# A token-routed layer in tiles: six sets of tile buffers and a first group of one chunk

## The reference

```python
x = x + attn_a(layernorm(x))        # delta rule, a scan over the tokens
x = x + ffn(layernorm(x))
x = x + attn_b(layernorm(x))        # linear attention, in chunks, with a running state
x = x + ffn(layernorm(x))

def ffn(x):                         # 8 experts, 128 -> 256 -> 128, the best two of each token
    probs = softmax(x @ Wg); topw, topi = top_k(probs, 2); topw = topw / sum(topw)
    combine = sum(one_hot(topi, 8) * topw[..., None])
    y = relu(x @ W1[e]) @ W2[e]     # for every expert e
    return sum_e(combine[:, e] * y[e])
```

## Time and profile before

| | us |
|---|---|
| median of 3 runs (828.03 to 835.17) | 830.47 |
| the profiled execution, device time | 829.9 |
| its span, first to last instruction | 828.2 |
| PE busy of the span | 650.5 |
| DVE busy | 623.2 |
| POOL busy | 487.7 |
| ACT busy | 483.2 |

### The profile page before, as it was taken

One profiled execution on the slowest core, in us unless ns is written; L12 is line 12 of the kernel. 1 busy time (PEld: TensorE's weight loads), 2 busy tenths in 40 slices (PEclk: granted clock), 3 DMA queues, 4 the chain that ended last, 5 costly groups with the idle time before them and its releaser, 6 DMA issues.

```text
span 828.2 us, 16746 instructions
## 1 busy us (share of the span) xinstructions
PE 650.5 (79%) x5108; PEld 534.2 (64%) x5108; DVE 623.2 (75%) x1648; ACT 483.2 (58%) x1266; POOL 487.7 (59%) x552
## 2 busy tenths in 40 slices
PE   4744265998989899686755979998999999787694
PEld 3423143877767778475652757886888778677594
DVE  4598989999999999999995685776678766352314
ACT  3974457697897969473634451736447354523363
POOL 2029888697988989899285040621571337503665
PEclk9957575899999999989985888999999999999997
DMA  6330220404022040310102022434453354545641
GB/s 208 79 93 13 67 64 3 115 15 130 15 53 90 0 118 13 95 37 0 64 2 89 2 80 81 124 113 124 115 159 102 90 156 115 160 134 159 175 131 63
DMA packets 102077, 71.35 MB, mean 86 GB/s; under 512 B 44528, under 2 KB 89840, under 8 KB 101744
## 3 DMA queue, kind: packets, MB, share of 16 engines
q1 hardware_dynamic: 97392, 60.96, 25.9%
q0 software_dynamic: 4608, 9.45, 3.9%
HBM read 43.89 MB, written 26.48 MB: 85 GB/s over the span
## 4 chain that ended last, share of the span: by engine, by line
DVE 36%; PE 29%; issue 11%; SPq 9%; DMA 8%; ACT 4%; POOL 2%; DVEq 0%; POOLq 0%; ACTq 0%
DVE u L2510 7%; PE bank L1993 5%; DVE hist_mem L2515 5%; DVE hist_mem L2519 4%; DVE prod_mem L2503 4%; PE bank L2057 3%; PE bank L1959 2%; DMA kk<-in_w 2%; PE bank L2078 2%; SPq L613 2%; PE bank L1920 2%; DVE x L2651 2%; PE bank L1704 2%; DMA wv_part<-in_w 2%; SPq L616 2%
## 5 line engine op out<-in xcount | busy, mean ns | idle before, releaser
L1795 PE MATMUL bank<-w,hid 128*128 128x128 f32 x768 | 108.9, 302 | 31.8 <-DVE y_even L2651 18.3
L1795 PEld LDWEIGHTS bank<-w,hid 128*128 128x128 f32 x768 | 103.0, 214 | 43.1 <-issue 12.8
L863 POOL TENSOR_TENSOR oq_mem<-hist_mem,q_t 128x384 f32<-128x384 f32 (+1 forms) x96 | 101.4, 1091 | 0.0
L2510 DVE TENSOR_REDUCE u<-prod_mem 128x32 f32<-128x288 f32 x128 | 86.8, 678 | 3.4
L1145 ACT ACTIVATE hid<-bank 128x512 f32<-128x512 f32 x112 | 62.6, 598 | 26.4 <-PE bank L1775 25.5
L946 POOL DMA_INDIRECT sig<-s_ys,back_at x40 | 39.3, 983 | 60.7 <-DMA s_ys<-q_t 45.5
L931 POOL DMA_INDIRECT s_xs<-xf,row_at x40 | 40.3, 1007 | 53.4 <-DVE row_at L2955 42.6
L1704 PE MATMUL bank<-xnT_h,wtap_h 128*128 128x512 f32 x104 | 49.9, 480 | 20.3 <-DVE qkv L2475 10.2
L2519 DVE TENSOR_REDUCE hist_mem<-hist_mem 128x64 f32<-128x320 f32 x128 | 62.4, 487 | 3.4
L1993 PEld LDWEIGHTS bank<-v_bd,prod_mem 128*64 128x64 f32 x1024 | 59.3, 140 | 7.0 <-issue 5.9
L1993 PE MATMUL bank<-v_bd,prod_mem 128*64 128x18 f32 x1024 | 61.8, 214 | 0.1
(11 more groups left out here) (296 smaller groups left out, 1799.7 us busy)
## 6 DMA issues: line engine op xcount, KB each, us to landing
kk<-in_w SPq DMA_DIRECT2D x53, 128.0 KB
pin<-s_xs SPq DMA_DIRECT2D x104, 64.0 KB
wv_part<-in_w SPq DMA_DIRECT2D x51, 128.0 KB
s_qkv<-qkv SPq DMA_DIRECT2D x24, 256.0 KB, 3.4
pin<-s_qkv SPq DMA_DIRECT2D x16, 256.0 KB, 2.8
s_ys<-q_p SPq DMA_DIRECT2D x26, 128.0 KB
s_ys<-q_t SPq DMA_DIRECT2D x26, 128.0 KB
q_p<-s_qkv SPq DMA_DIRECT2D x8, 256.0 KB, 2.7
```

The lines of the kernel that those rows point to most:

```text
L863: tt(oq[:, :, j, :, 0:HD], s_at, bc(turned[:, n, j], 2, HD), ALU.mult).then_inc(o_part, 1)
L1795: last = nc.tensor.matmul(bank[:, y_bank(e, wide), tokens], hid[:, e % 2, f, tokens], w2[:, e, f], start=(f == 0), stop=(f == FC - 1))
L2510: red(u[:, n], prod[:, n].rearrange("p m e j -> p m j e"), AX_X, ALU.add).then_inc(step, 1)
```

## The change

The groups become (6), (7, 8), (9, 10), (11, 12), (13, 14): five instead of four, of 8, 12, 12, 12 and 12 pairs, 56 in all. `BUFFERS` goes from 3 to 6, so the load of pair p waits for `tile_up(p - 6)`; the new buffers lie in `hid` and `y_even`, which the dense passes use, and the loads of pairs 2 and 4 wait until those are free. Inside `tile_load` the wait for the buffer now stands behind the two loads of registers. And all engines' lists after the delta-rule stage are written in a new order.

```diff
-GROUPS = ((6, 7), (8, 9), (10, 11, 12), (13, 14))
+GROUPS = ((6,), (7, 8), (9, 10), (11, 12), (13, 14))
...
-        BUFFERS = 3
+        BUFFERS = 6
...
-        xs = [pin_mem[:, D * k:D * (k + 1)] for k in range(2 * BUFFERS)]
-        w1_tile = [(kk_mem, part_mem)[k // 3][:, FF * (k % 3):FF * (k % 3 + 1)] for k in range(2 * BUFFERS)]
+        even_mem = y_even[:].rearrange("p j d -> p (j d)")
+        xs = [pin_mem[:, D * k:D * (k + 1)] for k in range(8)] + [even_mem[:, D * k:D * (k + 1)] for k in range(4)]
+        hid_mem = hid[:].rearrange("p h f t -> p (h f t)")
+        w1_tile = [(kk_mem, part_mem)[k // 3][:, FF * (k % 3):FF * (k % 3 + 1)] for k in range(4)] + [
+            hid_mem[:, FF * k:FF * (k + 1)] for k in range(8)]
...
-                if p >= BUFFERS:
-                    sp.wait_ge(tile_z, p - BUFFERS + 1)
                 _, at = nc.values_load_multi_w_load_instructions(
...
                     skip_runtime_bounds_check_because=EXPERT_WHY)
+                if p >= BUFFERS:
+                    sp.wait_ge(tile_z, p - BUFFERS + 1)
+                elif p == 2:
+                    sp.wait_ge(y_part, E * N1)
+                elif p == 4:
+                    sp.wait_ge(added, EV * N1)
...
             lin_turn(0)
-            place(6)
             lin_project(0)
             lin_values(0)
+            place(6)
...
+            tile_load(25)
+            tile_load(26)
+            tile_load(27)
+            store_sparse(7)
+            tile_store(20)
+            load_mid(6)
...
-            moe_add(6, 3)
-            gather(14)
+            gather(14)
+            moe_add(6, 3)
```

More of the change, by code:

```diff
@@ L1551, in _ @@
             tile_relu(21)
+            lin_outT(4)
+            lin_v(5)
+            lin_heads(5, 1)
             tile_take(20)
+            lin_rstdf(12)
+            lin_ktok(5, 0)
             tile_copy(23)
             tile_relu(22)
+            moe_xfT(12)
+            tile_take(21)
+            tile_copy(24)
+            lin_ktok(5, 1)
+            tile_relu(23)
+            tile_take(22)
+            tile_copy(25)
+            moe_exp(12)
+            tile_relu(24)
+            lin_rstd(6)
@@ L2184, in _ @@
             tile_up(7)
+            lin_ktok(2, 0)
+            lin_ktok(2, 1)
+            lin_scores(2, 0)
+            moe_transpose(9)
+            tile_down(6)
+            moe_route(9)
+            lin_scores(2, 1)
+            lin_numer(2, 0)
+            place(9)
+            tile_turn(9)
+            tile_up(8)
+            tile_down(7)
+            lin_scores(2, 2)
             lin_numer(2, 1)
@@ L2319, in _ @@
             tile_down(24)
+            lin_numer(5, 1)
+            lin_turn(6)
+            lin_scores(5, 3)
+            lin_numer(5, 2)
+            lin_project(6)
+            lin_state(5, 0)
+            lin_numer(5, 3)
             tile_turn(27)
-            lin_scores(6, 1)
-            lin_numer(6, 0)
             tile_up(26)
-            place(13)
+            lin_transpose(5)
+            lin_state(5, 1)
+            lin_project_out(5)
+            lin_values(6)
             tile_down(25)
@@ L2327, in _ @@
             tile_up(27)
+            lin_state(5, 2)
+            tile_down(26)
+            tile_turn(29)
+            moe_transpose(13)
+            tile_up(28)
+            tile_down(27)
+            lin_ktok(6, 0)
+            moe_route(13)
+            tile_turn(30)
+            tile_up(29)
+            lin_ktok(6, 1)
+            lin_scores(6, 0)
+            tile_down(28)
+            place(13)
+            tile_turn(31)
+            tile_up(30)
+            tile_down(29)
+            tile_turn(32)
+            tile_up(31)
+            lin_scores(6, 1)
+            lin_numer(6, 0)
             lin_scores(6, 2)
@@ L2332, in _ @@
             lin_numer(6, 3)
[L2333 to L2352 removed]
             tile_down(30)
             tile_turn(33)
+            lin_transpose(6)
             tile_up(32)
[L2356 to L2357 removed]
+            lin_project_out(6)
             tile_down(31)
+            lin_state(6, 0)
             tile_turn(34)
@@ L2425, in _ @@
             tile_down(49)
+            tile_turn(52)
             tile_up(51)
             tile_down(50)
+            tile_turn(53)
+            tile_up(52)
+            tile_down(51)
+            tile_turn(54)
+            tile_up(53)
+            tile_down(52)
+            tile_turn(55)
+            tile_up(54)
+            tile_down(53)
+            tile_up(55)
+            tile_down(54)
+            tile_down(55)
+            moe_route(15)
             dense_up(6, 0)
-            tile_down(51)
             dense_up(6, 1)
@@ L3169, in _ @@
             lin_out(5, 2)
+            lin_state(5, 0)
+            lin_phi_low(6)
             lin_out(5, 3)
-            lin_phi_low(6)
-            lin_state(5, 0)
             lin_phi(6)
@@ L3201, in _ @@
             gates(14)
+            table(4)
+            back(4)
+            lin_phi_low(7)
             lin_state(6, 1)
+            lin_phi(7)
             lin_state(6, 2)
@@ L3205, in _ @@
             lin_att(7, 1)
-            table(3)
-            back(3)
             lin_out(7, 0)
-            combine(8)
             lin_att(7, 2)
```

753 lines of the change are left out of this document (356 added, 397 removed).

## The result

The changed kernel takes 799.1 us (median of 4; 797.6 to 801.9) against 829.8 us (median of 4; 828.0 to 835.2): 0.9624 of the time before, with a 95% interval of 0.957 to 0.9677. The forecast was 811, its range 801 to 828. So the direction was right and the gain was larger than the range allowed: 30.7 us where I had said 19.

A forecast was written before the change was run, and what follows sets the result against it. PE was taken to bound the kernel from 440 us, its idle time being winnable, with SP's queue setting the pace behind P. P at 704.0, plus 67 to D, plus 39.3 to the end made 810.3, forecast as 811 us, range 801 to 828.

The forecast's parts named there:

- Part 1: Up to P, the last `place`: P moves from 711.8 to 704.0 us, by gains less moved work and new waits.
- Deeper ring: PE, 500 us to P: six sets let loads lead further, so of 12.3 us of load waits 9.3 go.
- New waits: PE, 500 us to P: it arrives earlier at the same steps, so 3.1 us of DVE and ACT waits double, +3.
- Earlier first tiles: PE, about 484.6 to 500 us: first tiles go in earlier and fill holes in 3.2 us of idle, -2.
- First steps: PE at the start: `lin_project(0)` no longer stands behind the 4.05 us wait for `place(6)`, -3.
- Moved work: PE before P: more tile work comes ahead (7.2 us), some chunk steps go behind (-3.7), net +3.5.
- Rival C: Loads don't lead, since SP's stores wait for `tile_take` ahead of them; load waits stay: 833 us, chance 0.08.
- Part 2: From P to D, the start of pass 15: SP's path (64.7 us) is later than PE's (60.7); taken as 67.
- Part 3: From D, the start of pass 15, to the end: 39.3 us against 39.8 before.
- A: Before P, PE's waits only change name, to a chunk's chain through PE, DVE and ACT: 821 us, chance 0.20.
- B: Slower: pass 7, now in the second group, comes late for `load_mid(6)` and PE's `lin_turn(6)`: 838 us, chance 0.08.
- The hidden loads: Behind P, six sets hide the loads wholly and PE's path of 60.7 us sets the time: 804 us, chance 0.12.

## Why the prediction was too small

**Part 1 failed.** It had P 7.8 us earlier, and P came 28.9 us earlier. Of the missing 21.1 us, 7.6 belong to "Deeper ring" with "New waits", 5.9 to "Earlier first tiles" with "First steps", 5.9 to "Moved work", and 1.7 to the scatter of where state step 0 begins. The step that failed is the same in all three: I priced each part by the waits of before, as if it stood alone, and at the clock of before.

**"Earlier first tiles", -2 us, and "First steps", -3.** I priced the new start as two holes. The wait for `place(6)` was worth nothing by itself in the trace of the old order: taken out, the next wait, for DVE, grew from 3.2 to 5.64 us. The new order of the first two steps makes the start 14 us shorter on its own, and all of it is lost again when no tiles stand behind it (0.9947, P unmoved). In the changed kernel PE has tiles at 468 us in place of 500, from the first group of one chunk, which I took for 3.2 us of idle and no more. Up to 500 us the idle time fell by 10.9 us and not by 5. That the start needs something behind it is shown. That the group of one is what it needs is argued: the changed kernel also has the ring and a new order behind the start, and a run with the group of one alone wasn't made.

**"Deeper ring" and "New waits"**, -9.3 and +3, made -6.3 of idle time from 500 us to P; it was -13.9. I had left 3 us of load waits and doubled the rest. There were none of the first, and the others went as well, from 3.1 us to 1.5. My reason for doubling, that PE arrives earlier at the same steps, was wrong in its sign. I read it so: with up to six pairs at hand the order has a tile to put into each step of the chunk's chain. The ring cut to four shows that the depth has its part, 5.8 us of idle time to P. Rival C is what happened where the ring was put into the old order with the later `place`: SP's waits in stores went from 14.7 to 31.4 us and most of the load waits remained. Neither half gives much where the kernel before takes 830 us: ring and `place` in the old order 0.9924, the start and the ring 0.9864, new order with four sets 0.9966, all of it 0.9624. How much the ring alone would give there is open, since on the other chips it gave 10 to 13 us in the old order too.

**"Moved work", +3.5**, was +3.5 of work at the clocks of before, but PE's busy time to P fell by 2.4. The granted clock explains it at least in part, and this stands for 5.9 of the missing 21.1 us: 0.75 from 434.1 to 482.7 us and 0.80 up to 500 before, 0.80 and 1.00 after. `lin_project(1)` alone took 3.53 us before and 1.88 after. No term of mine had the clock in it.

**Part 2.** The mechanism was right, SP's path is the later one, and its size was not. I had 64.7, took 67, and it was 75.7. In the terms of the sum: 20.7 us to the first load and not 15, 44.5 for the twelve loads and their stores and not 43, 10.5 from there to D and not 6.7. The first term failed at "`pads(4)` fits before". The last scatter was issued by 12.6 us behind P, as forecast (12.75), but the pads stand in SP's list behind the loads of pairs 42 and 43 and were issued from 12.1 to 16.9 us behind P, with four stores after them. The last term was too small even without any wait for results (10.4 us with the stores on ACT). PE's waits for results, 7.4 us, I hadn't counted at all; but the run that took them away got waits for loads in their place and no shorter way (78.6 us). What did shorten the way was taking stores out of SP's queue, 68.9. PE's own path was 66.0 us of busy time, where I had 60.7.

**The rule weighed.** By the Trainium skill, DMA: Bandwidth & Descriptors, section "Issuing engines are not separate DMA queues", the sequencer's time to start a DMA is usually small beside the DMA. For one transfer the trace agrees: 0.43 us of issue on SP, and the last data of before were used 2.7 us after their issue. By that rule the loads would be hidden wholly, and up to P they were, with no wait for a load left. Behind P they weren't: a pair's steps add up to 3.05 us on SP, an eighth of the weight bytes changed nothing (76.0 us), and nine stores fewer took 5.5 us off the twelve loads.

**Part 3** was right, 39.4 against 39.3, and by its own steps: POOL's first add ended 24.6 us behind D (forecast 24.3), and PE's last `dense_down` came 2.65 us late (3). **The other rivals:** A didn't come: between 467 us and P no wait on DVE or ACT is above 0.9 us. Waits did change their name behind P, but to the result buffers, which is not the chain of a chunk that A meant. B didn't come: no wait of `lin_turn(6)` shows. The hidden loads (804 us) came nearest in time, by another way.

## What to carry to other kernels

- Price an early hole together with what PE does behind it. Here a shorter start that ran into steps with nothing to fill them was waited off again, at a lower clock; in the changed kernel, with tiles ready behind it, it was kept.
- A deeper ring is worth what the issuing queue lets through. Look in that queue for what stands ahead of the loads and can wait (stores, pads), and count its steps (issues and loads of registers), not its bytes. If a wait moves from results to loads when you add buffers, look at the queue that issues both, and try one kind of transfer on another engine.
- Parts of a change that feed each other can't be summed from the waits of before. Where each part removes the limit on the next, the range must reach to where nearly all idle time is gone: here 31.4 us of it to P fell to 6.6.

## What the runs showed of the hardware

On three chips the kernel before took 972 us and on the others 830; the changed one took 960 us on one of the three, and 799 elsewhere. Up to 430 us the two traces of the changed kernel agree within 2 us (the turn of step 0 at 433.7 and at 432.4). Behind it the program is straight-line code, and there PE has many waits that end with nothing that the profile shows ("issue"). The largest of them in the changed kernel on such a chip; with the smaller ones they come to 74.6 us behind the turn of step 0, where the trace from the other chips has none:

```profile
PE bank L2076 <- issue: 21.9, 5, 11.5
...
PE bank L1789 <- issue: 17.3, 2, 16.2
...
PE bank L2021 <- issue: 13.6, 18, 1.2
```

In order of time, single matmuls 0.7 us apart that elsewhere run in a row:

```profile
551.74 0.18 PE L2021 MATMUL bank<-v_bd,prod_mem 128*64 128x18 f32 x1 [0.52 <-issue]
552.46 0.29 PE L2021 MATMUL bank<-v_bd,prod_mem 128*64 128x18 f32 x2 [0.54 <-issue]
553.17 0.18 PE L2021 MATMUL bank<-v_bd,prod_mem 128*64 128x18 f32 x1 [0.42 <-issue]
```

The instruction queues moved the same there (39 packets and 0.64 MB, 39 and 0.32) in the same share of the time, 0.3% and 0.1%. I take it that instructions reach the engines late, but no run shows it, and why only on some chips stays open. It matters for what is compared: there the changed kernel gained 1.5% and not 3.8%, and cutting its ring to four changed nothing on the way to P (322.6 us and 322.5), while elsewhere it cost 9.6 us.
